# A two-layer graph network on one core: rings of eight for the last layer's rows, loaded by GpSimd, and finer update units from block 28 on

## What is computed

```python
# layer 0
m = silu(concat([x[src], x[dst], edge_attr]) @ msg_W1 + msg_b1) @ msg_W2 + msg_b2
agg = segment_sum(m, dst)
h = silu(concat([x, agg]) @ upd_W1 + upd_b1) @ upd_W2 + upd_b2
x = layernorm(x + layernorm(x + h) * gamma + beta)
# layer 1
agg = segment_sum(x[src], dst) / max(degree, 1)
h = relu(relu(concat([x, agg]) @ W1 + b1) @ W2 + b2)
out = layernorm(x + h)
```

## Time and profile before

| | |
|---|---|
| median of 3 runs | 2214.85 us (2213.88 to 2218.34) |
| span of the profiled execution | 2215.4 us |
| PE busy | 1979.7 us (89%) |
| DVE busy | 1662.3 us (75%) |
| POOL busy | 1515.0 us (68%) |
| ACT busy | 1432.8 us (65%) |
| chain that ended last | POOL 46%, PE 18%, issue 17%, DMA 8%, DVE 6% |

### The profile page before, as it was taken

One profiled execution on the slowest core, in us unless ns is written; L12 is line 12 of the kernel. 1 busy time (PEld: TensorE's weight loads), 2 busy tenths in 40 slices (PEclk: granted clock), 3 DMA queues, 4 the chain that ended last, 5 costly groups with the idle time before them and its releaser, 6 DMA issues.

```text
span 2215.4 us, 59812 instructions
## 1 busy us (share of the span) xinstructions
PE 1979.7 (89%) x19664; PEld 1740.5 (79%) x19664; DVE 1662.3 (75%) x5615; ACT 1432.8 (65%) x3734; POOL 1515.0 (68%) x1605
## 2 busy tenths in 40 slices
PE   7888888889988998999998999999989999999774
PEld 7877777777887887887886898987987998988542
DVE  7688877877886877887887788888887788774332
ACT  3677766776776766776776777766766766673122
POOL 7577777777777777777777777777777777770110
PEclk9999989997998997998999999999998999999976
DMA  8477767676687777777877787877877887986822
GB/s 288 139 206 219 201 189 213 175 220 202 187 231 211 210 218 210 216 239 231 241 232 210 241 249 243 269 238 219 254 244 227 272 266 238 293 264 207 268 65 62
DMA packets 307523, 487.82 MB, mean 220 GB/s; under 512 B 120202, under 2 KB 181644, under 8 KB 307208
## 3 DMA queue, kind: packets, MB, share of 16 engines
q10 hardware_dynamic: 102369, 251.46, 34.3%
q1 hardware_dynamic: 154823, 129.94, 19.8%
q0 software_dynamic: 50016, 102.53, 17.9%
HBM read 375.62 MB, written 108.13 MB: 218 GB/s over the span
## 4 chain that ended last, share of the span: by engine, by line
POOL 46%; PE 18%; issue 17%; DMA 8%; DVE 6%; ACT 2%; DVEq 1%; ACTq 0%; SPq 0%; POOLq 0%
POOL gath L858 46%; DMA gath<-P_d,src_i 6%; PE ps_l L1167 4%; PE ps_pre L1114 3%; PE ps_cnt L1131 3%; DVE edgeK L917 2%; PE ps_sum L1151 2%; DMA gath<-x1T_d 1%; DVE pre L930 1%; PE ps_pre L1225 1%; DVE edgeL L915 1%; ACT eT_c L1401 1%; PE ps_pre L1227 1%; PE ps_pre L1117 1%; PE ps_p L432 1%
## 5 line engine op out<-in xcount | busy, mean ns | idle before, releaser
L858 POOL DMA_INDIRECT gath<-P_d,src_i x1535 | 1456.8, 949 | 486.9 <-issue 455.7
L917 DVE TENSOR_SCALAR edgeK<-iotaK,key 128x500 bf16<-128x500 f16 (+1 forms) x1564 | 667.3, 488 | 0.0
L1114 PE MATMUL ps_pre<-wc,eT_c 128*128 128x128 f32 x3128 | 613.7, 318 | 2.4 <-issue 2.4
L1131 PE MATMUL ps_cnt<-edgeK,edgeL 128*128 128x250 bf16 (+1 forms) x3128 | 479.9, 301 | 92.4 <-ACT counts L1269 48.6
L1114 PEld LDWEIGHTS ps_pre<-wc,eT_c 128*128 128x128 f32 x3128 | 508.8, 204 | 25.0 <-issue 2.6
L1269 ACT ACTIVATE counts<-ps_cnt 128x1000 bf16<-128x1000 f32 x391 | 404.4, 1034 | 173.2 <-issue 85.1
L1151 PE MATMUL ps_sum<-edgeN,h 128*128 128x40 f32 x3128 | 421.8, 285 | 55.4 <-ACT h L1325 55.1
L1151 PEld LDWEIGHTS ps_sum<-edgeN,h 128*128 128x128 f32 x3128 | 391.6, 196 | 81.1 <-ACT h L1325 69.1
L930 DVE TENSOR_TENSOR pre<-ps_pre,gath 128x512 f32<-128x512 f32 x384 | 260.9, 680 | 254.9 <-DMA gath<-P_d,src_i 175.7
L1131 PEld LDWEIGHTS ps_cnt<-edgeK,edgeL 128*128 128x128 bf16 x3128 | 288.3, 101 | 162.1 <-DVE edgeK L917 83.4
L1325 ACT ACTIVATE h<-pre 128x512 f32<-128x512 f32 x391 | 243.9, 624 | 262.4 <-DVE pre L930 258.6
(11 more groups left out here) (160 smaller groups left out, 1505.5 us busy)
## 6 DMA issues: line engine op xcount, KB each, us to landing
eT_c<-eT ACTq DMA_DIRECT2D x193, 512.0 KB
A_d<-counts ACTq DMA_DIRECT2D x168, 384.0 KB
rel_c<-rel_d ACTq DMA_DIRECT2D x193, 240.0 KB
A_v<-A_d SPq DMA_DIRECT2D x70, 448.0 KB
A_v<-A_d SPq DMA_DIRECT2D x111, 256.0 KB
gath<-P_d,src_i POOLq DMA_INDIRECT x1535
A_d<-counts ACTq DMA_DIRECT2D x56, 416.0 KB
Qw<-Q_d SPq DMA_DIRECT2D x56, 180.0 KB
```

What stands on the lines that cost most here:

```text
L858: pool.indirect_dma_start(gath[:, q, t * D:(t + 1) * D], None, v["P_d"], bass.IndirectOffsetOnAxis(ap=src_i[g % 2][:, c:c + 1], axis=0)).t ...
L917: last = V.tensor_scalar(edgeK[x][:, ROFF[j]:ROFF[j] + A2 * w], iotaK[j][:, :, 0:A2 * w // KR], key[k][:, q * QT + j:q * QT + j + 1], None ...
L1114: T.matmul(o, eT_c[c % RE][:, e0:e0 + P], wc[:], start=True, stop=False)
L1131: last = T.matmul(o[:, :, w0:w0 + w], edgeL[x][:, j, 0:P], r, start=(j == 0), stop=(j == QT - 1 and q == 0), skip_group_check=True)
```

## The change

Three things are changed.

- The rings for the last layer's rows are eight long (`RL`), and their buffers are spread over tiles that the edge loop no longer needs: seven slices of `gath` and `xT_u` for `xT_l`; halves of `eT_c`, the two `h`, `hT_u`, `z_u` and `xT1_u` for `x_l`. The ring of results `z_l` stays at three (`RZ`).
- `load_last` moves from ACT to GpSimd. Behind its last gather GpSimd starts eight loads (two DMAs each), of which the first five wait for the unit of their blocks and the last three for all units. Then it goes on with the means; load w + 6 stands behind mean w, for w = 2 to 6, and waits for k0 and k3 of unit w - 2.
- From block 28 on (`FINE`) the update units of layer 0 have two blocks. There are 17 units instead of 13, starting at steps 246, 260, 281, 295, 309, 330, 344, 358 and 372 in place of 260, 295, 330, 358 and 372. The planner then makes 443 visits instead of 432, with the same 2744 blocks: 456 blocks in 86 visits fall at step 392 or later, and the last visit at step 425 instead of 430.

```diff
-UB, LAST_B = 4, 46
+UB, LAST_B, FINE = 4, 46, 28
+RL, RZ = 8, 3
-        hi = min(lo + UB, LAST_B)
+        hi = min(lo + (UB if lo < FINE else 2), LAST_B)
...
-    xT_l, x_l = [gath[:, i, :] for i in range(3)], [gath[:, 3 + i, :] for i in range(3)]
+    xT_l = [gath[:, i, :] for i in range(GQ)] + [xT_u]
+    x_l = [t[:, UB * D:2 * UB * D] for t in eT_c] + [t[:].rearrange("p t n -> p (t n)") for t in h] + [
+        hT_u, z_u[:].rearrange("p j n -> p (j n)"), xT1_u]
...
+        def load_last(w):
+            cols, n = last_columns(w)
+            r = w % RL
+            if w == 0:
+                pool.wait_ge(pre_add, NQ)
+                pool.wait_ge(sum_mm, NQ)
+            u = next(u for u, (b0, b1, s0) in enumerate(UNITS) if LAST_UNITS[w][1] <= b1)
+            if r >= 5:
+                u = len(UNITS) - 1
+            pool.wait_ge(x1_out, 16 * (u + 1))
+            pool.wait_ge(x1T_out, 16 * (u + 1))
+            if w >= RL:
+                pool.wait_ge(l_hidden, w - RL + 1)
+                pool.wait_ge(l_z, w - RL + 1)
+            pool.dma_start(xT_l[r][:, 0:n * P], v["x1T_d"][:, cols]).then_inc(l_xT_in[r], 16)
+            pool.dma_start(x_l[r].rearrange("p (j n) -> p j n", n=D)[:, 0:n, :],
+                           v["x1_d"][cols, :].rearrange("(j p) n -> p j n", p=P)).then_inc(l_x_in[r], 16)
...
+            for w in range(RL):
+                load_last(w)
             for w in range(len(LAST_UNITS)):
...
                 nc.gpsimd.tensor_tensor(sumT[:, cols], sumT[:, cols], deg[:, cols], ALU.mult).then_inc(l_mean, 1)
+                if w >= 2 and w + RL - 2 < len(LAST_UNITS):
+                    load_last(w + RL - 2)
...
-                if w + 3 < len(LAST_UNITS):
-                    load_last(w + 3)
...
-                if s == UNITS[-1][2] + U_LEN + 1:
-                    for w in range(3):
-                        load_last(w)
```

More of the change, by code:

```diff
@@ L712, in build_edges @@
     a_in = [sem(f"av_in{r}") for r in range(RT)]
-    l_xT_in, l_x_in, l_out = ([sem(f"l_{n}{i}") for i in range(3)] for n in ("xT_in", "x_in", "out"))
+    l_xT_in, l_x_in = ([sem(f"l_{n}{i}") for i in range(RL)] for n in ("xT_in", "x_in"))
+    l_out = [sem(f"l_out{i}") for i in range(RZ)]
     l_mean, l_hidden, l_relu, l_y, l_z, l_var, l_sd, l_rs, l_norm, l_dv = (
@@ L829, in fast @@
             sp.wait_ge(dg_io, 64 * len(UNITS))
-            for r in range(3):
-                sp.wait_ge(l_out[r], 16 * len(range(r, len(LAST_UNITS), 3)))
+            for r in range(RZ):
+                sp.wait_ge(l_out[r], 16 * len(range(r, len(LAST_UNITS), RZ)))
         def general(sp):
@@ L1028, in last_step @@
                 n, x = last_columns(w)[1], w % 2
-                z = z_l[w % 3].rearrange("p (j n) -> p j n", n=D)[:, 0:n, :]
+                z = z_l[w % RZ].rearrange("p (j n) -> p j n", n=D)[:, 0:n, :]
                 dve.wait_ge(l_y, w + 1)
[L1031 to L1034, removed]
+                if w >= RZ:
+                    dve.wait_ge(l_out[w % RZ], 16 * (w // RZ))
+                dve.wait_ge(l_x_in[w % RL], 16 * (w // RL + 1))
+                V.scalar_tensor_tensor(z, ps_y[x][:, 0:n * D].rearrange("p (j n) -> p j n", n=D), 0.0,
+                                       x_l[w % RL].rearrange("p (j n) -> p j n", n=D)[:, 0:n, :], ALU.max,
                                        ALU.add).then_inc(l_z, 1)
@@ L1223, in last_step @@
                     pe.wait_ge(l_relu, w - 1)
-                pe.wait_ge(l_xT_in[w % 3], 16 * (w // 3 + 1))
-                T.matmul(o, w1[:, 0, :], xT_l[w % 3][:, 0:n * P], start=True, stop=False)
+                pe.wait_ge(l_xT_in[w % RL], 16 * (w // RL + 1))
+                T.matmul(o, w1[:, 0, :], xT_l[w % RL][:, 0:n * P], start=True, stop=False)
                 pe.wait_ge(l_mean, w + 1)
@@ L1363, in unit_step @@
                 A.activation(xT1_u[:, 0:n * P], ps_u[:, 0:n * P], ACT.Copy).then_inc(u_xT, 1)
[L1365 to L1378, removed]
         def last_step(w, k):
@@ L1397, in last_step @@
                 n, x = last_columns(w)[1], w % 2
-                z = z_l[w % 3].rearrange("p (j n) -> p j n", n=D)
+                z = z_l[w % RZ].rearrange("p (j n) -> p j n", n=D)
                 act.wait_ge(l_rs, w + 1)
@@ L1404, in last_step @@
                 act.dma_start(v["out"][last_columns(w)[0], :].rearrange("(j p) n -> p j n", p=P),
-                              z[:, 0:n, :]).then_inc(l_out[w % 3], 16)
-                if w + 3 < len(LAST_UNITS):
-                    load_last(w + 3)
+                              z[:, 0:n, :]).then_inc(l_out[w % RZ], 16)
         def fast():
```

## The result

| | before | changed |
|---|---|---|
| median of 4 runs each | 2214.67 us (2213.88 to 2218.34) | 2165.77 us (2159.80 to 2167.86) |
| span of the profiled execution | 2215.4 us | 2166.0 us (its own time 2167.86) |

The changed kernel takes 0.9775 of the time (95% interval 0.9759 to 0.9792). The forecast was 2159.3; the time lies 6.5 us above it and inside the range.

What follows compares the result with a forecast made beforehand. The tail was taken as bound by a loop through a ring of three, the edge loop by GpSimd and, at its end, PE. Gains 7.5 + 0.8 + 37.9 + 9.4 = 55.6 from 2215.4 gave 2159.8, median 2159.3 us; range 2147 to 2180.

Steps and rivals of the forecast that it cites:

- term A: End of the edge loop: finer units let blocks be done earlier, gaining 7.5 us, range 0 to 10.
- Term B: First visits after the loop: counts come in one DMA instead of three, gaining 0.8 us, range 0 to 1.6.
- Term C: From step 405's first visit to the last add: 76.1 us instead of 114.0, paced by DVE, a gain of 37.9.
- Term D: From the last add to the last normalise: 30.6 us instead of 40.0, a gain of 9.4.
- the loop through a ring of three: Tail: ACT normalises a unit, then starts the load three units on; PE stands 35.2 us before k0 for loads.
- the cover: Edge loop, steps 246 to 344: extra units' cost hides under gathers; if that is gone, it is 5 us.
- 4.4 us for seams: Up to the last add: allowance because a bank waits for its add and a k3 for its k2.
- GpSimd's loads: Load starts on GpSimd's queue, from its last gather through the means: taken to cost 0, bound + 5 us.
- The bound of 5.35 us a load: GpSimd's queue: upper estimate of a load's two DMAs at the gather's price, 43 us for eight loads.
- rivals 2 and 5: Loads on GpSimd's queue hold back means: 2172, chance 0.08; over 18.6 us a load, slower, about 2222, chance 0.02.
- The stretch to 3.1 us: GpSimd's DMA starts slowed by DVE, 620 ns alone against 3100: first mean some 10 us late, about + 4.
- Rival 1: Tail: PE stays at the lower clock or seams are wider, 2169 to 2175 us; chance 0.2.

Runs made afterwards that it cites:

- e1: Rings of eight loaded by GpSimd, with the whole four-block units of before, against the changed kernel: 2174.0 us, ratio 0.9819 to before.
- e2: Kernel of before, rings of three loaded by ACT, with only the finer units from block 28 added: 2217.23 us, ratio 1.0021 to before.
- e3: Changed kernel with ACT starting the loads, eight at step 402 and w + 8 behind the store of w: 2165.65 us, ratio 0.9796 to before.
- e4: Changed kernel with GpSimd starting three loads instead of eight, and load w + 3 behind mean w: 2170.83 us, ratio 0.9807 to before.
- e5: Changed kernel planning only whole or step-filling visits behind the last quad, 14 adds fewer, on the slower chip: 3040.79 us, ratio 0.9893 to before.
- e13: Changed kernel with whole visits, plan_last prices of 0.8 and 4.5 us, and two-block units only from block 40: 2162.55 us, ratio 0.9755 to before.
- e6: Changed kernel with plan_last prices of 0.8 us a visit and 4.5 us between last units, on the slower chip: 3039.23 us, ratio 0.9882 to before.
- e9: Changed kernel run once more, unaltered, on the slower chip: 3043.20 us, ratio 0.9862 to the kernel of before there.

## Why the prediction held, term by term

The sum went from 2215.4 to 2159.8, and the span is 2166.0. The misses are 0.7 (term A) + 2.8 (B) + 0.5 (C) + 2.3 (D) - 0.1 (what follows the last normalise, 8.1 us in place of 8.2) = 6.2.

**What bounded the kernel** was named rightly: the loop through a ring of three. e1 shows it alone.

**Term A, 7.5 predicted, 6.8 measured** (the last unit's first product, 2018.09 to 2011.26). The size is no proof of the reasoning. With units fine from 28 on the last silu started at 2005.2, 2009.5, 2002.3 and 2013.3 (changed, e2, e3, e4; mean 2007.6), with whole units at 2011.3 and 2009.5 (before, e1; mean 2010.4). That is some 3 us, with single executions 5 us either side, so that a gain by the units at the loop's end is not shown. The mechanism was there, since the lag grows by less from quad 364 to 385. The step that failed is "cost nothing as long as the lag is caught up before step 364": I took the cover as given and left the 5 us to a clause, and in e2 and e4 it was gone.

**Term B, 0.8 predicted, -2.0 measured** (35.2 to 37.2). The counts did come sooner (a wait of 1.30 in place of 1.56 us), so that part is right in kind. The step that failed is "is the same work in the same order, and moves as a block": other kernels with this stretch unchanged took 34.1 to 37.2 us. A spread of 3 us in a stretch of 35 had to stand in the sum as a bound.

**Term C, 76.1 predicted, 76.6 measured.** The size is right, the make-up less. I had DVE set the pace throughout and 4.4 us for seams. In the first part it was PE: 20.00 busy of 20.00 at 2060 to 2080 us, at a granted clock of 0.87, and of the idle time before the adds, 21.1 us went to the add before and 16.6 to PE's products. DVE's groups by line, from 2048.4 to 2125 us:

```profile
L974 DVE TENSOR_TENSOR sumT<-ps_l,sumT 128x120 f32 x70 | 19.8, 283 | 40.3 <-DVE sumT L974 21.1 <-PE ps_l L1195 16.6 <-issue 2.6
```

So an argument by adds alone overrates what fewer adds bring, and e5 showed it (6.7 us for fourteen). In e13 PE is busy for 66.0 of the 71.9 us of C, so I take it for the next bound; no run tests that.

One thing in C stood nowhere in my sum. The second instruction of k5 on DVE (L1077) takes 0.16 us in eleven of the thirteen units, and took 1.80 and 2.85 in the other two. Each time it ended as means on GpSimd ended, at 2105.5 and 2117.7 us. Timelines of DVE, of POOL (the second row is four means in a row), and of PE behind the second hold:

```profile
2103.75 1.80 DVE L1077 SCALAR_TENSOR_TENSOR shift_l<-mv_l,rs_l 128x4 f32<-128x4 f32 x1
...
2114.83 2.85 DVE L1077 SCALAR_TENSOR_TENSOR shift_l<-mv_l,rs_l 128x4 f32<-128x4 f32 x1
```

```profile
2104.25 1.28 POOL L890 TENSOR_TENSOR sumT<-sumT,deg 128x512 f32<-128x512 f32 x1
...
2112.72 4.94 POOL L890 TENSOR_TENSOR sumT<-sumT,deg 128x512 f32<-128x512 f32 x4
```

```profile
2119.33 0.37 PE L1195 MATMUL ps_l<-edgeK,x1h 128*128 128x120 bf16 x4 [1.79 <-DVE sumT L974]
```

The adds that stood behind the held instruction came late, and PE waited 1.79 us for one of them. In e3 and e4, where L1077 never took over 0.43 us, PE waited 0.18 at this place, and their C is 2.2 and 2.0 us shorter. So C came near my sum with some 2 us in it that I did not know of. The means came in a row because GpSimd had them behind the load of unit 12, which waits for k3 of unit 4. In e5 L1077 took 1.81 and 4.01 us, so part of what its fourteen adds did not bring may lie here too.

**Term D, 30.6 predicted, 32.9 measured.** Four-block units came 4.7 us apart in place of 4.5, some 1 us over five of them. The rest I put down to the time about the last add: k2 of unit 6 and k0 of unit 7 ran at the lower clock (2.07, 2.08 and 1.92 us, where 1.12, 1.16 and 1.02 stand for the later ones). What D is worth depends on C: its gain of 7.1 against before is a balance. I did not say that the units' part of C comes back in D, since `plan_last` moves last units behind the visits as visits go. e1 and the changed kernel put numbers on it, 10.9 gained and 9.4 returned. My sum had both terms for the whole change and came out right, but read by halves, it would have told a wrong price for the units.

**GpSimd's loads, 0 predicted.** The bound of 5.35 us a load was far off: the row of the gather, 0.95 + 0.30, was the nearer one. Timeline of POOL behind the last gather, the two DMAs of the first load, the first of the sixth, the first mean, and a load behind the third mean:

```profile
2010.57 0.57 POOL L867 DMA_DIRECT2D gath<-x1T_d  x1 [15.47 <-issue]
2011.13 0.80 POOL L868 DMA_DIRECT2D eT_c<-x_d  x1
2011.90 0.57 POOL L867 DMA_DIRECT2D gath<-x1T_d  x1
...
2046.47 0.54 POOL L867 DMA_DIRECT2D gath<-x1T_d  x1 [29.32 <-DMA x1T_d<-xT_u]
...
2053.66 1.27 POOL L890 TENSOR_TENSOR sumT<-sumT,deg 128x512 f32<-128x512 f32 x1 [3.35 <-DVE sumT L974]
...
2075.41 0.57 POOL L867 DMA_DIRECT2D gath<-x1T_d  x1 [12.29 <-DVE eT_c L1061]
```

A load holds the queue 1.3 us. The first mean waited for an add, not for a load. With that, rivals 2 and 5 are refuted in their price, and what e3 did with ACT in GpSimd's place bears it out. But 0 was not the whole of it: later loads did hold back the means behind them, and these held DVE (term C). The stretch to 3.1 us did not show: the DMAs took 0.54 to 0.80 us, also while DVE added. That is no test of the rule, though: the Trainium skill (SBUF — State Buffer, "Who interferes with whom") has it for DVE's two-port modes, and says that `tensor_tensor`, which the adds are, has none.

**Rival 1**, the lower clock or wider seams, held in D for one unit only, and C came out near its sum at a granted clock of 0.90. Behind that one slow stretch the waits were 0.78 us each, and k0 stayed at 1.02.

## What to carry to other kernels

A prefetch is only as far ahead as the last thing that its start waits for: with the same units, starting load w + 3 from the mean of w instead of behind the store of w (e4 against e2) took 50 us out of a tail of 158, while the engine and eight loads in place of three changed nothing that could be told. Ask of every saving what fixed order stands behind it: with last units placed by a planner, eight adds less were 10.9 us before the last add and -9.4 behind it, and two prices set to what was measured gave back 8 of the tail's 109 (e6). And where a stretch is to "move as a block", take its spread from more than one execution (here 3 us of 35, and 5 of the loop's end) before setting bounds.

## What the runs showed of the hardware

**A small DVE instruction can be held by GpSimd's work.** k5's L1077 reads two tiles of the on-chip memory; it took 0.16 us alone, and up to 2.85 us beside GpSimd's means (changed) and 4.01 (e5). In fourteen traces every instance over 0.3 us overlaps a mean and ends within 0.04 us of a mean's end, and no shorter one overlaps any. The 1.80 began 0.5 us before its mean, while GpSimd started a load's second DMA (2103.47 to 2104.23). The adds beside it, with one operand from PE's sums, stayed at 0.28 us.

**A start of a plain DMA on GpSimd is short:** 0.54 to 0.58 us for 128 rows of 512 numbers, 0.75 to 0.80 us for 4 x 128 rows of 128, beside 0.95 + 0.30 for an indirect one. On ACT's queue the same starts were not always shorter. e3, timeline of ACT, loads 0 and 4:

```profile
2040.84 0.33 ACTq L1384 DMA_DIRECT2D gath<-x1T_d  x1
2041.19 0.46 ACTq L1385 DMA_DIRECT2D eT_c<-x_d  x1
...
2047.36 2.30 ACTq L1384 DMA_DIRECT2D gath<-x1T_d  x1
```

**One chip ran the edge loop at another pace,** whichever kernel. e9, the changed kernel there, in the window 1000 to 1500 us (columns of the earlier trace rows), and the largest wait of DVE (us, times, longest):

```profile
1000.00:1500.00 500.00, 402.19 (x3188) 335.50 (x3186) 283.92 (x961) 251.84 (x654) 265.24 (x282) 0.78 0.53 156
```

```profile
DVE pre L957 <- remote: 717.7, 158, 12.9
```

In the profile of before 400 gathers fall in this window, at a PE clock of 0.96; here it is 282, at 0.78. A gather is no longer there (265.24 / 282 = 0.94 us). DVE waits, before it adds the gathered rows, for something that the profile doesn't name. What it is stays open; the tail, which has no gathers, took the same time on both.
